# Attention maxima over 32 queries of four heads at a time, on eighths of the array, and products issued in pairs of heads

## What is computed

```python
Q = _apply_rope(proj(W_q), positions, sin, cos)
K = _apply_rope(proj(W_k), positions, sin, cos)
V = proj(W_v)
scores = jnp.einsum('bhnd,bhmd->bhnm', Q, K) / jnp.sqrt(jnp.float32(D_K))
causal = jnp.tril(jnp.ones((S, S), dtype=bool))
scores = jnp.where(causal[None, None], scores, -jnp.inf)
attn = jax.nn.softmax(scores, axis=-1)
head = jnp.einsum('bhnm,bhmd->bhnd', attn, V)
```

## Time and profile before

| | |
|---|---|
| median of 3 runs | 1017.29 us (1016.52 to 1020.27) |
| span of the profiled execution | 1008.0 us; its own launch time is not listed |
| PE busy | 874.2 us (87%) |
| DVE busy | 816.2 us (81%) |
| ACT busy | 725.7 us (72%) |
| maxima alone (prologue of attention) | about 118 to 148 us |
| attention, 16 groups | about 148 to 537 us |

### The profile page before, as it was taken

The page is one execution under the profiler, slowest core; times in us unless marked ns, Lnnn a source line. Parts: engine busy times, 40 slices in busy tenths (PEclk is TensorE's granted clock), DMA queues, the critical chain, the costliest instruction groups (busy, mean ns, idle before and its releaser), DMA issues. The chain is left out here.

```text
span 1008.0 us, 25094 instructions
## 1 busy us (share of the span) xinstructions
PE 874.2 (87%) x9373; PEld 464.7 (46%) x9374; DVE 816.2 (81%) x1699; ACT 725.7 (72%) x1493; POOL 289.1 (29%) x331
## 2 busy tenths in 40 slices
PE   4999899899999999999898898778999999979960
PEld 3666543334333333333344666533444444458850
DVE  6665499899999999999923766589999999928895
ACT  2666408788888888888784454478999999948851
POOL 4865311111111000000003656500344443005560
PEclk9999859999999999999999888768999999989995
DMA  5579851644445353330004899695354643546637
GB/s 167 223 267 331 280 133 42 205 101 105 110 98 125 89 123 84 68 69 14 13 24 127 277 317 301 226 241 101 67 118 94 114 89 54 136 142 189 206 119 252
DMA packets 121560, 147.20 MB, mean 146 GB/s; under 512 B 19213, under 2 KB 81242, under 8 KB 120800
## 3 DMA queue, kind: packets, MB, share of 16 engines
q1 hardware_dynamic: 116064, 133.74, 48.0%
q0 software_dynamic: 5376, 11.85, 4.1%
HBM read 77.63 MB, written 69.54 MB: 146 GB/s over the span
## 5 line engine op out<-in xcount | busy, mean ns | idle before, releaser
L854 ACT ACTIVATE probsB<-psB 128x512 f32<-128x512 f32 (+2 forms) x640 | 310.0, 566 | 87.1 <-PE psB L928 61.5
L766 DVE TENSOR_REDUCE mxB<-psB 128x1 f32<-128x512 f32 (+2 forms) x448 | 256.9, 642 | 11.1 <-PE psB L892 8.3
L921 PE MATMUL psB<-q_groups,k_groups 64*128 64x512 bf16 (+3 forms) x768 | 205.8, 330 | 16.6 <-DVE mxB L766 8.3
L892 PE MATMUL psB<-k_groups,q_groups 64*128 64x512 bf16 (+3 forms) x768 | 217.0, 344 | 2.8 <-PEq L293 1.7
L959 PE MATMUL psB<-probsB,vB 128*32 128x512 f32 (+3 forms) x1536 | 164.5, 500 | 0.7 <-ACT probsB L854 0.5
L1725 ACT ACTIVATE psD<-psD 128x896 f32<-128x896 f32 (+2 forms) x192 | 153.4, 799 | 12.9 <-PE psD L1779 12.7
L921 PEld LDWEIGHTS psB<-q_groups,k_groups 64*128 64x128 bf16 x768 | 67.5, 94 | 161.2 <-ACT probsB L854 140.3
L1656 DVE TENSOR_REDUCE sumsD<-psD 128x1 f32<-128x128 f32 (+3 forms) x256 | 113.2, 481 | 11.8 <-PE psD L1802 9.4
L899 PE MATMUL psB<-hideB,chooseB 64*128 64x128 bf16 (+1 forms) x1024 | 115.1, 210 | 0.0
L1779 PE MATMUL psD<-k_groups,q_groups 64*128 64x512 bf16 (+3 forms) x384 | 104.4, 343 | 12.3 <-ACT psD L1725 5.6
L766 DVE TENSOR_REDUCE mx2B<-psB 128x1 f32<-128x384 f32 (+2 forms) x192 | 104.4, 594 | 8.5 <-PE psB L899 6.9
(11 more groups left out here) (227 smaller groups left out, 1504.5 us busy)
## 6 DMA issues: line engine op xcount, KB each, us to landing
v<-vaugA SPq DMA_DIRECT2D x4, 2048.0 KB, 8.9
vB<-v SPq DMA_DIRECT2D x16, 512.0 KB
q_groups<-q SPq DMA_DIRECT2D x32, 200.0 KB
k_groups<-k SPq DMA_DIRECT2D x32, 200.0 KB
q_groups<-q SPq DMA_DIRECT2D x32, 192.0 KB
k_groups<-k SPq DMA_DIRECT2D x32, 192.0 KB
back<-emptyB POOLq DMA_DIRECT2D x16, 256.0 KB, 3.8
o<-outB SPq DMA_DIRECT2D x128, 32.0 KB, 1.8
```

The source lines that it names most:

```text
L766: nc.vector.tensor_reduce(dst, src, AX.X, ALU.max).then_inc(max_read, 1)
L854: nc.scalar.activation(probs[:, n % DEEP, 0:w], st[n % BANKS][:, 0:w], ACT.Exp, scale=DH ** -0.5).then_inc(exp_done, 1)
L892: ins = nc.tensor.matmul(bank[:, to:to + w], q[half[r], s, hq // 2, t * P:t * P + P], k[half[r], s, hq // 2, HALF * c:HALF * c + w], start ...
L921: ins = nc.tensor.matmul(bank[:, to:to + w], k[half[r], s, hq // 2, jt * P:jt * P + P], q[half[r], s, hq // 2, i0:i0 + w], start=True, sto ...
```

## The change

Row tiles of 32 queries take the place of blocks of 128. A PSUM bank holds, on its 128 partitions, 32 queries of each of the four heads; a unit has four matmuls of 64 rows by 32 columns of the array (`heads_of`), and two units (f = 0 and 1) take the array's eight such tiles. The keys of a unit end at a multiple of 32. `kinds` lists 20 pairs; four of them (`None`) join two short row tiles in one bank. The mask is one matmul of 32 moving columns per half of the rows, with a stationary tile of 64 by 64. There are again 40 units a group. The second table of maxima (`mx2B`) goes.

Even steps issue the scores of two steps side by side, one on each half of the rows, with both waits in front; after them comes `maxima` with two units. Odd steps issue only a PV where one is due. The maxima are placed by 16 DMAs in place of two, each of 16 pieces of 32 elements.

```diff
+ROW_TILE = 32
...
+    kinds = [(5, 0), (13, 1), (14, 0), (2, None), (1, None), (15, 0), (7, 0), (15, 1), (8, 0), (9, 0), (4, 0), (12, 1), (0, None),
+             (3, None), (10, 0), (6, 0), (11, 0), (14, 1), (12, 0), (13, 0)]
...
+    def first_row(f, t):
+        return ROW_TILE * (t if ROW_TILE == 64 else 2 * t + f)
+
+    def max_width(f, t, c):
+        return min(HALF, first_row(f, t) + ROW_TILE - HALF * c)
+
+    def heads_of(f, r):
+
+        return [(2 * f + r, 64 * (r ^ f))] if ROW_TILE == 64 else [(2 * a + r, 64 * (r ^ f) + ROW_TILE * a) for a in range(2)]
...
+    units = [(f, t, c) for t, c in kinds for f in range(2)]
...
-        LOADS, PLACED, STORED, SOURCES = 16 * 5, 16 * 2, HEAD_STORES, 16 * 4
+        LOADS, PLACED, STORED, SOURCES = 16 * 5, 16 * 8 * (64 // ROW_TILE), HEAD_STORES, 16 * 4
...
                     for part in range(2):
-                        sp.dma_start(q[AUG + part:AUG + part + ROWS + 1:ROWS, x % QUADS, :, :],
-                                     neg[32 * part:32 * part + 32, x % 2, :]).then_inc(neg_placed[x % 2], 16)
+                        for f in range(2):
+                            for r in range(2):
+                                row, src = ROWS * r + AUG + part, slice(32 * part + 16 * f, 32 * part + 16 * f + 16)
+                                for hq, at in heads_of(f, r):
+                                    dst = q[row:row + 1, x % QUADS, hq // 2, :]
+                                    dst = dst.rearrange("p (t i) -> p t i", i=ROW_TILE) if ROW_TILE == 64 else (
+                                        dst.rearrange("p (t f i) -> p f t i", f=2, i=ROW_TILE)[:, f])
+                                    sp.dma_start(dst, neg[src, x % 2, at:at + ROW_TILE]).then_inc(neg_placed[x % 2], 16)
...
                     def score(i):
...
+                        ti, ci = segments[i]
+                        w = max_width(f, ti, ci)
+                        last = first_row(f, ti) // HALF > ci
+                        for r in range(2):
+                            for hq, at in heads_of(f, r):
+                                ins = nc.tensor.matmul(bank[at:at + ROW_TILE, w * i:w * i + w],
+                                                       q[half[r], s, hq // 2, first_row(f, ti):first_row(f, ti) + ROW_TILE],
+                                                       k[half[r], s, hq // 2, HALF * ci:HALF * ci + w], start=True, stop=last)
...
+                    def causal(i):
+                        ti, ci = segments[i]
+                        to = max_width(f, ti, ci) * (i + 1)
+                        for r in range(2):
+                            at = 64 * (r ^ f)
+                            ins = nc.tensor.matmul(bank[at:at + 64, to - ROW_TILE:to], choose[half[r], 0, 0:64], hide[half[r], :],
+                                                   start=False, stop=True)
...
+                def maxima(*both):
+
+                    for i in range(both[0][0]):
+                        for n, score, _ in both:
+                            if i < n:
+                                score(i)
+                        for n, _, causal in both:
+                            if causal and i < n:
+                                causal(i)
...
                     for e, (j, heads) in enumerate(steps):
-                        both = [for_products(x, e)]
-                        if todo and todo[0][1] is None:
-                            turn_over(todo.pop(0)[0])
-                        if todo:
-                            both.append(for_maximum(*todo.pop(0)))
-                        side_by_side(*both)
+                        if e % 2 == 0:
+                            side_by_side(for_products(x, e), for_products(x, e + 1))
+                            if todo and todo[0][1] is None:
+                                turn_over(todo.pop(0)[0])
+                            if todo:
+                                maxima(*[for_maximum(*todo.pop(0)) for _ in range(2)])
```

More of the change, by code:

```diff
@@ L100, in __init__ @@
         self.loaded = [m.sem(f"groups_loaded{s}") for s in range(QUADS)]
-        self.masks = [m.sb(n, [P, 2, P], BF16) for n in ("chooseB", "hideB", "hide_laterB")]
+        self.masks = [m.sb(n, shape, BF16) for n, shape in (("chooseB", [P, 2, P]), ("hideB", [P, ROW_TILE]), ("hide_laterB", [P, 2, P]))]
         self.masks_loaded = m.sem("masks_loaded")
@@ L592, in attention @@
     slots = [(0, 0), (0, 1), (0, 3), (0, 2), (1, 0), (1, 2), (1, 4), (1, 5), (1, 3), (1, 7), (1, 6), (1, 1)]
-    tiles = [(2, 0), (4, 0), (0, 0), (1, 0), (5, 0), (3, 0), (6, 1), (4, 1), (5, 1), (6, 0), (7, 0), (7, 1)]
-    def packs(w):
-        return [(0, 2), (1, 3)] if 2 * w <= HALF else [(hq,) for hq in range(4)]
-    def max_width(t, c):
-        return min(HALF, P * (t + 1) - HALF * c)
+    kinds = [(5, 0), (13, 1), (14, 0), (2, None), (1, None), (15, 0), (7, 0), (15, 1), (8, 0), (9, 0), (4, 0), (12, 1), (0, None),
+             (3, None), (10, 0), (6, 0), (11, 0), (14, 1), (12, 0), (13, 0)]
     def slot_width(j):
@@ L604, in slot_width, with packs, row_tile, parts_of @@
         return HALF * (c + 1) - max(HALF * c, P * jt)
-    units = [(tuple(hq ^ 1 for hq in heads), t, c) for t, c in tiles for heads in packs(max_width(t, c))]
+    def packs(w):
+        return [(0, 2), (1, 3)] if 2 * w <= HALF else [(hq,) for hq in range(4)]
+    def row_tile(f, t):
+        return 16 * f + t if ROW_TILE == 64 else 2 * t + f
+    def first_row(f, t):
[4 more added lines that the diff above has]
+        return [(2 * f + r, 64 * (r ^ f))] if ROW_TILE == 64 else [(2 * a + r, 64 * (r ^ f) + ROW_TILE * a) for a in range(2)]
+    def parts_of(f, t, c):
+        return [(t, 0), (t + 8, 1)] if c is None else [(t, c)]
+    units = [(f, t, c) for t, c in kinds for f in range(2)]
     steps = [(j, heads) for j in range(len(slots)) for heads in packs(slot_width(j))]
-    assert [max_width(t, c) for _, t, c in units[16:] + units[:16]] == [slot_width(j) for j, _ in steps]
+    assert len(units) == len(steps)
     UNITS, SLOTS_B = len(units), len(slots)
@@ L757, in _ @@
                         continue
[L758 to L762, removed]
[L763 to L765 removed]
+                    f, t, c = units[g]
+                    w = max_width(f, t, c or 0)
+                    if c is None:
+                        dst, src = mx[:, par, :, f, t], mxb[n % RING][:, 0:2 * w].rearrange("p (a w) -> p a w", w=w)
+                    else:
+                        dst, src = mx[:, par, c, f, t - 8 * c:t - 8 * c + 1], mxb[n % RING][:, 0:w]
                     nc.vector.tensor_reduce(dst, src, AX.X, ALU.max).then_inc(max_read, 1)
@@ L814, in split_maxima @@
                     pool.wait_ge(combined, x + 1)
-                    nc.gpsimd.tensor_scalar(lower, mx[:, par, :, :, :].rearrange("p a b t -> p (a b t)"), -1.0, None,
+                    nc.gpsimd.tensor_scalar(lower, mx[:, par, 0, :, :].rearrange("p f t -> p (f t)"), -1.0, None,
                                             ALU.mult).then_inc(split, 1)
@@ L880, in for_maximum @@
                     s = x % QUADS
-                    heads, t, c = units[g]
-                    w = max_width(t, c)
+                    f, t, c = units[g]
                     if n >= RING:
@@ L886, in for_maximum @@
                         pe.wait_ge(in_loaded[s], LOADS * (x // QUADS + 1))
-                    bank = mxb[n % RING]
+                    bank, segments = mxb[n % RING], parts_of(f, t, c)
                     def score(i):
[L890 to L894, removed]
-                            ins.then_inc(max_done, 1)
@@ new lines, in score @@
+                        if last:
+                            ins.then_inc(max_done, 1)
+                    def causal(i):
[5 more added lines that the diff above has]
+                                                   start=False, stop=True)
+                        if i == len(segments) - 1:
@@ L990, in _ @@
                     else:
-                        side_by_side(for_maximum(x, g))
+                        maxima(for_maximum(x, g))
                 waiting = []
@@ L2243, in constants @@
     choose = np.where(p[None, None, :] == row, 1.0, 0.0)
-    hide = np.where(p[None, None, :] > row, MASKED, 0.0)
+    hide = np.where(np.arange(ROW_TILE)[None, :] > p[:, None] % ROW_TILE, MASKED, 0.0)
     hide_later = np.where(p[None, None, :] < row, MASKED, 0.0)
```

7 lines of the change are left out of this document (4 added, 3 removed).

## The result

The changed kernel takes 1213.96 us (1208.13 to 1217.35, 5 runs) against 1017.29 us (1015.41 to 1021.15 in the same session): 1.192 times as long, 95% interval 1.189 to 1.196. I forecast 1100 us, with a range of 1060 to 1142. The sign was right and the size was less than half of it: +197 us where +82.5 was worked out.

A forecast was written before the change was run, and what follows sets the result against it. DVE was taken to lead the kernel before. PE's line 27.7 + copy 0.7 + placing 0.5 = 28.9 us a group against 23.84, 70 us over 14 groups; with prologue and last groups +82.5, to 1100 us, range 1060 to 1142.

The forecast's parts named there:

- order of PE's work: PE's products, maxima, PV and tile changes in line, each iteration at least its floor: 27.7 us a group, 0.7 for keep.
- waiting for the placed maxima: At each group's start, the first product waits 0.4 to 0.8 us for the last placed row; 0.5 added.
- prologue, groups 14 and 15: Stretches outside the 14 steady groups: prologue +6 us (+3 to +10), group 14 +3.5, group 15 +3.
- Placing the maxima: On SP, sixteen DMAs at 0.46 us an issue take 7.4 us, last row landing 9.2 to 9.6 after the cast.
- rival 3: Placing is the bound: 0.53 to 0.57 us an issue adds 1.1 to 1.8 a group, total 1115 to 1125; chance 0.08.
- rival 5: PE's clock falls as it streams less; half of attention at 1.2 GHz gives above 1200 us; chance 0.04.
- output copy: `keep(x, 0)` in ACT at pair k = 8 waits for that iteration's PV and delays k = 10 by 0.7 us.
- loops from pair to pair: Time from one product pair to the next, the larger of PE work and exponentials' floor: 1.00 to 1.83 us.
- the ring: Three exponentials' banks with paired waits leave one exponential outstanding, not two: a floor of 22.9 us a group.
- fewer columns: DVE's reduces read 16896 columns a group, 1536 fewer, in the same 40 reduces: -1.6 us a group.

The follow-up runs named there:

- e1: Changed kernel with the first 28 units of a group, not 16, computed one group early, so maxima are cast six pairs earlier: 1121.70 us, ratio 1.107.
- e2: Changed kernel with 44 added matmuls on mask data in front of each group's wait for the placed maxima: 1182.79 us, ratio 1.168.
- e3: Kernel before with only the pairing: products issued in pairs with both waits in front, then two units of maxima: 1080.76 us, ratio 1.067.
- e4: Changed kernel with row tiles of 64 queries of two heads instead of 32 of four, and 8 placing DMAs: 1096.62 us, ratio 1.084.
- e5: Kernel of e3 with each step of a product pair waiting for its own bank right before its own matmuls: 1058.08 us, ratio 1.037.
- e6: Kernel of e1 with the maxima's mask as four matmuls of 64 by 32 array tiles instead of two of 64 by 64: 1114.87 us, ratio 1.094.
- e7: Kernel before with the maxima placed by 16 DMAs of 8 pieces of 128 B in place of 2: 1132.19 us, ratio 1.111.
- e8: Changed kernel with the edits of e1 and e6 and the own waits of e5: 1108.96 us, ratio 1.087.

## Why the prediction was right in its sign and wrong in its size

The 198 us between the spans, with what the runs give for each part:

| | forecast | measured | from |
|---|---|---|---|
| order of PE's work, 14 groups | +4.6 each | +6.1 each, 85 us | e1's undisturbed 29.94 against 23.84 |
| waiting for the placed maxima | +0.5 | +4.7, 66 us | e2 (34.67 mean) against e1 |
| clock after that wait | 0 | at least +1.7, 23 us | changed kernel (36.34) against e2 |
| prologue, groups 14 and 15 | +6, +3.5, +3 | +9.2, +8.5, +3.0 | rows above |

Before rounding the rows add to 196; they take 23.84 for the kernel before, whose mean is 23.98, which makes them 2 too much, and 4.5 lie after attention. The split between the first two rows is as good as e1 is the changed kernel without its wait; it also has the maxima in another order against the products. A second way gives nearly the same: the first nineteen pairs of the group shown of e2 take 28.30, and with 1.14 to 1.51 for the twentieth the order of PE's work costs 5.6 to 6.0. Of the second row about 0.5 a group belongs to the third, as said under e2: 4.2 for the wait and 2.2 for the clock.

**Placing the maxima: the step that failed.** I priced a DMA of sixteen pieces by the stores, 0.46 us an issue, with bounds of 0.35 and 0.53. It is 0.63, outside them. The nearest row was there: the two DMAs of the placing itself, with on-chip memory at both ends as the new ones have, took 1.05 us, 0.55 from the first to the second. I halved the 1.05 and called it the upper bound, though no row said that an issue of this kind gets cheaper with fewer pieces. Even rival 3's 16 x 0.57 = 9.1 us would have given too little. Of the 2.5 us that are missing to 11.6, 1.0 is 0.63 against 0.57 and 1.5 are the two slow issues of this placing. The trace before had such issues too, 9 among the 182 of SP between 200 and 484 us, for instance this load:

```profile
251.79 1.32 SPq L118 DMA_DIRECT2D k_groups<-k  x1
```

I left them out of the price. Since cast to landing was already past the edge of its cover, the work of the pairs k = 14 to 19 that runs meanwhile (9.2 to 9.6 against 8.8), every tenth of a microsecond on an issue went into the time in full, sixteen times a group: issuing takes 4.0 us more than the 7.4 of the forecast, and PE waits about 4 us longer a group than the 0.5. The mechanism is that of rival 3, but its price of 1.1 to 1.8 us a group was too low as well, since its 0.53 to 0.57 an issue lie under 0.63.

**The clock: the mechanism that I had apart from its cause.** I gave the fall of the clock 4 in 100, as something that PE's thinner stream might bring by itself. The runs show the tie: with the wait, 4 to 11 us at half clock in each group (clock 0.86 to 0.94 from group 1 to 13); without it (e3, e4, and all but two groups of e1) 1.00 from group 1 to 13, though PE streams about as many columns in a group; with the wait filled by work (e2) 1.00. So rivals 3 and 5 were one case, not two. The Trainium skill has this in "TensorE: Matmul & The Clock Gate", section HAM oscillation: a wait for a DMA between two bursts of matmuls brings the lower clock back for the next burst. The trace agrees: 4.6 us of standing, then 1.2 GHz for the first iterations. That the time came out above 1200, where rival 5 has it, is chance: it priced half of attention at 1.2 GHz at 8 us a group, and the clock took about 2.

**The order of PE's work: right, 5% short.** With its output copy it was forecast at 28.4 us a group and took 29.94 in e1. The loops from pair to pair were forecast as 1.23, 1.00, 1.31, 1.14, 1.14, 1.23, 1.07, 1.00 and 1.31 for k = 1, 4, 5, 7, 9, 11, 13, 16, 17; e2's group has 1.24, 1.17, 1.21, 1.21, 1.30, 1.24, 1.10, 1.17, 1.21. Those with a PV of 512 columns were 1.71 to 1.83 for k = 10, 12, 14, 15 and 18 and came to 1.76 to 1.90. The largest misses are k = 2 and 3 together (3.42 forecast, 2.25 + 1.41 measured), k = 19 (1.14, and 1.51 in e1 where nothing waits), and k = 4 and 16. In k = 2 stands the output copy `keep(x-1, 1)`, which the sum left out; the one that I priced, at k = 8, came out right (1.87 against 1.21 + 0.7). e3 has 2.10 + 1.41 there with large tiles, so at most 0.15 comes from the small ones; that it is the copy was not tried by itself.

**The pairing and the tiles.** Pairing alone costs 4.4 us a group (e3). Of that the ring is at least 1.7 (e5), and the rest, at most 2.7, is by exclusion work in line. The small tiles add 1.7 more in e1 (29.94 against 28.20). The changes of tile shape inside the maxima are 1.2 of these (e6, quietest groups), 0.06 for each of the twenty, as some of them are hidden; one that shows costs the 0.10 us that I took from the earlier trace rows.

**DVE.** Its busy time in a group fell from 22.62 to 22.2 us, where about 20.9 was forecast, and it no longer leads. Of the 1.6 us expected from fewer columns only 0.4 shows in busy time. I read that as the pipeline's end of each reduce, which busy time counts where a reduce stands alone; no run tests it.

**Prologue and group 14.** The prologue's cast came only 1.7 us later than before (144.17 against 142.46), where 6 less the 2.5 for placing leaves 3.5 in the forecast; the other 7.5 of the 9.2 are the placing, 13.8 us from cast to exponential against 6.3. Here too the step that failed is the placing. Group 14 was forecast at +3.5 and took +8.5. It lasts 31.7 us in e3, 34.0 in e2 at full clock and 35.9 in the changed kernel at a clock of 0.79, against 27.3: the pairing alone is 4.4 of it and the clock about 1.9.

## What to carry to other kernels

Count the DMAs of a hand-over and price each by a DMA of the same kind that is in the trace, from one start to the next and with the slow ones among them, then look at what covers the chain: once it is longer than its cover, every further issue is paid in full and by all engines, and PE's clock may follow. When work of two rings is issued in pairs, write down how many results may be outstanding before and after; an in-order engine also pays for what was side by side and now stands in line. A saving on the engine that leads counts only as long as it leads.

## What the runs showed of the hardware

A DMA from SyncE between two places in on-chip memory costs its queue 0.67 us from one to the next for 8 pieces of 128 B (e7), 0.63 for 16 of 64 B (changed kernel) and 0.55 for 32 of 256 B (kernel before), with mostly one or two slower ones of 0.8 to 2.4 us in a row of sixteen. Matmuls on eight tiles of 64*32 take 0.41 us, two on 64*128 with the same 512 columns 0.39. The changes of tile shape between 64*128, 64*32, 64*64 and 128*32 cost 0.09 to 0.12 us at full clock, also where the rows stayed the same. After standing for 3.7 to 6.8 us PE was at 1.2 GHz for 4 to 11 us of the group, in e7 as in the changed kernel; after stands of 1.6 to 2.4 us in e8 the clock fell for some us in part of the groups and not in the others.
